# A DLRM tower on one core: transposes of both tiles in a row, then both Grams, with layer matmuls among them

## The chip, the cores and the metric

The kernel runs on one core of a Trainium2 chip. Its engines run side by side and meet through semaphores: PE (matrix products), DVE and ACT (element-wise work and evictions from PSUM), POOL (here it issues gathers) and SP (here it issues the other DMAs). The metric is the time of one execution on the device in microseconds (us), lower is better.

## What is computed

For each of 2048 rows of the batch, 27 ids each pick a row of 128 floats from a table of their own. The 27 vectors give all pairwise dot products (351), a dense context of 16 values is appended, and three layers follow:

```python
e = jnp.stack([tbl_0[ids[:, 0]], ..., tbl_26[ids[:, 26]]], axis=1)
dot = jnp.einsum('bnd,bmd->bnm', e, e)      # 27 x 27 per row of the batch
z = flat[:, idx]                            # its 351 entries below the diagonal
h = jnp.concatenate([z, dense_ctx], axis=1)
h = jnp.maximum(h @ W_top1 + b_top1, 0.0)   # 367 -> 512
h = jnp.maximum(h @ W_top2 + b_top2, 0.0)   # 512 -> 256
y = h @ W_top3                              # 256 -> 1
```

Ten of the tables have 1000 rows; the others have 1250, 12500 or 125000.

## The kernel before

The batch is worked off in eight pairs of tiles, a tile being 128 rows of the batch. `sweep` writes three bodies: pair 0 unrolled, a hardware loop over pairs 1 to 6 (its passes), and pair 7 unrolled. A pair goes through these stages.

*Lookups.* The ten tables of 1000 rows (`NM`) live in SBUF as `parts`, a high and a low half of each float (`split_high` on ACT, `split_low` on DVE), and are read by a matrix product with a onehot of the ids. `make_onehot` builds one table's onehot in eight instructions from `ids_b`, mostly on DVE, for pair 0 partly on ACT (`ACT_ONEHOTS`). There are four onehot slots (`OH`), so tables 4 to 9 wait for lookups that free a slot. `lookup(p, k)` does two tables into one PSUM bank (five per pair), and ACT moves the bank to `embT`.

*Gathers.* The other 17 tables (`NG`) are gathered by POOL, 17 gathers of 128 rows per tile, at most two queued at a time, into `rows`. There is one buffer per tile, so the gathers of a group for pair p+1 wait until PE has transposed that group of pair p.

*Transposes.* The 17 blocks of a tile are transposed by PE in five groups (`TR`, of 4, 4, 4, 3, 2 blocks; `transpose_rows`) into the four `emb_ps` banks, which the lookups use too, and moved to `embT` by ACT (groups 0, 2, 4) and DVE (groups 1, 3).

*Gram.* `gram(p, t, s)` does half a tile's Gram matrices: 64 small products, into one bank per half. DVE copies the first half and ACT the second (`keep_blocks`), and DVE's `turn` makes `z` of a tile. PE transposes it (`transpose_z`), and the layers follow, one pair behind: in the loop they stand among the next pair's stages (`layers`). In the profile a float32 product counts as two records, each with its own weight load.

*SP* loads the tables, the weights, the ids of the onehots (`load_ids`: tables 0 to 3, then 4 to 9; each goes to all 128 partitions, 128 KB per table) and the ids of the gathers (`load_idx`, one per tile). In the loop the ids of tables 4 to 9 of the next pair are loaded when DVE has built this pair's ten onehots, and `load_idx(p + 1, 1)` when all rows of tile 1 have landed.

Each engine works its list in the order in which the code writes it; nothing reorders it. PE's list for a pair in the loop is: lookup 0, `transpose_z` of the pair before (tile 1), lookups 1 and 2, the first layer of the pair before, lookups 3 and 4; then per tile the five groups, a layer (the second beside tile 0, the third beside tile 1), a wait for the moves, and the Gram. `transpose_z` of tile 0 ends it.

## Time and profile before

| | |
|---|---|
| time, median of 3 runs | 417.63 us (416.83 to 418.69) |
| the profiled execution: time | 419.41 us |
| its span | 417.6 us |
| PE, DVE, ACT, POOL busy | 83%, 66%, 38%, 63% of the span |
| mean granted clock of PE | 0.95 |

The span is what the trace covers, from the first to the last instruction; the time has 1.8 us around it. "Idle before" in a row is the time its engine stood still ahead of the row, with what ended it; "issue" means that nothing which the profile shows held it. A pair's stage is best found by PE's first lookup of the pair, at 80.98, 128.91, 172.43 and so on to 352.15 us for pairs 1 to 7.

### The profile page before, as it was taken

How to read it: one execution, taken by the hardware profiler on the slowest of the kernel's cores; microseconds unless marked ns; L12 is line 12 of the kernel's file. 1: busy time of each engine (PE TensorE's matmuls, PEld its weight loads, DVE VectorE, ACT ScalarE, POOL GpSimd, SP SyncE). 2: the span in 40 equal slices, each digit the busy share in tenths (PEclk: the TensorE clock that was granted, in tenths of full speed). 3: DMA queues.
4: the chain of work that ended last, by engine and by line, in shares of the span. 5: the costliest groups of instructions: out<-in, count | busy, mean ns of one | idle time of the engine just before them, and what ended most of it. 6: DMA issues, size and time to landing. Idle time of an engine off the chain costs nothing.

```text
span 417.6 us, 15062 instructions
## 1 busy us (share of the span) xinstructions
PE 348.4 (83%) x6092; PEld 312.5 (75%) x6092; DVE 276.0 (66%) x741; ACT 159.7 (38%) x221; POOL 262.4 (63%) x277
## 2 busy tenths in 40 slices
PE   0277686799979998899989998999899998899766
PEld 0266576689859897789778986898688976897565
DVE  0647954796765965896579677787479748952410
ACT  0827961223432334422442343334422334234422
POOL 5777417777477737677777767767777677770000
PEclk9978675999998999999999999999999999999889
DMA  4799995362425233245524352419333562210000
GB/s 82 176 254 249 222 82 85 65 99 64 99 54 110 52 74 84 58 90 71 113 58 102 58 111 52 109 32 85 98 75 82 66 108 56 54 53 14 3 3 0
DMA packets 29611, 35.51 MB, mean 85 GB/s; under 512 B 12729, under 2 KB 23617, under 8 KB 29586
## 3 DMA queue, kind: packets, MB, share of 16 engines
q1 hardware_dynamic: 20882, 17.32, 26.6%
q0 software_dynamic: 8704, 17.84, 15.7%
q8 instruction: 18, 0.29, 0.3%
q14 instruction: 7, 0.06, 0.0%
HBM read 35.13 MB, written 0.01 MB: 84 GB/s over the span
## 4 chain that ended last, share of the span: by engine, by line
PE 61%; DVE 12%; issue 10%; DMA 7%; ACT 6%; SPq 4%; ACTq 0%; DVEq 0%
PE emb_ps L579 26%; PE gram_ps L602 13%; DVE onehot L474 10%; PE mlp_ps L628 9%; PE mlp_ps L636 6%; DMA blocks<-in_tbl 4%; ACT embT L366 4%; PE emb_ps L591 3%; DMA ids_b<-in_ids_mm 3%; SPq L223 2%; PE mlp_ps L664 2%; PE mlp_ps L669 1%; DVE embT L480 1%; PE mlp_ps L612 1%; ACT h L408 1%
## 5 line engine op out<-in xcount | busy, mean ns | idle before, releaser
L333 POOL DMA_INDIRECT rows<-in_tbl,idx x272 | 262.1, 964 | 113.5 <-DMA rows<-in_tbl,idx 76.8
L474 DVE TENSOR_SCALAR onehot<-ids_b,row_of 128x256 fp32r<-128x256 int32 x616 | 188.5, 381 | 40.4 <-PE emb_ps L579 25.1
L579 PE MATMUL emb_ps<-onehot,parts 125*128 125x256 f32 x1280 | 171.4, 295 | 35.4 <-ACT parts L345 24.0
L579 PEld LDWEIGHTS emb_ps<-onehot,parts 125*128 125x128 f32 x1280 | 163.9, 200 | 40.1 <-ACT parts L345 24.7
L362 ACT ACTIVATE embT<-emb_ps 128x512 f32<-128x512 f32 x40 | 48.0, 1216 | 107.3 <-PE emb_ps L579 107.3
L602 PE MATMUL gram_ps<-embT 128*32 128x26 f32 x4096 | 56.8, 198 | 20.0 <-issue 11.6
L602 PEld LDWEIGHTS gram_ps<-embT 128*32 128x32 f32 x4096 | 47.7, 112 | 33.8 <-issue 28.3
L480 DVE COPY embT<-emb_ps 128x512 f32<-128x512 f32 (+1 forms) x32 | 31.2, 1052 | 32.2 <-PE emb_ps L591 32.2
L591 PE MATMUL emb_ps<-ident,rows 128*128 128x128 f32 x272 | 40.4, 294 | 8.1 <-ACT embT L366 7.7
L366 ACT ACTIVATE embT<-emb_ps 128x512 f32<-128x512 f32 (+1 forms) x48 | 44.6, 1076 | 1.1 <-PE emb_ps L591 1.1
L591 PEld LDWEIGHTS emb_ps<-ident,rows 128*128 128x128 f32 x272 | 32.2, 150 | 13.6 <-ACT embT L366 6.7
L391 ACT ACTIVATE blocks<-gram_ps 128x416 f32<-128x416 f32 x16 | 14.5, 909 | 69.5 <-PE gram_ps L602 69.5
L628 PE MATMUL mlp_ps<-zT,w_sb 128*128 128x256 f32 (+1 forms) x168 | 37.5, 378 | 0.0
L628 PEld LDWEIGHTS mlp_ps<-zT,w_sb 128*128 128x128 f32 (+1 forms) x168 | 31.3, 189 | 4.2
L377 ACT ACTIVATE h<-mlp_ps,b_sb 128x256 f32<-128x256 f32 x42 | 17.6, 470 | 39.8 <-PE mlp_ps L628 22.2
L486 DVE COPY blocks<-gram_ps 128x416 f32<-128x416 f32 x16 | 14.0, 874 | 24.7 <-PE gram_ps L602 24.6
L494 DVE STREAM_TRANSPOSE turned<-blocks 128x832 f32<-128x832 f32 x16 | 16.6, 1040 | 14.3 <-ACT blocks L391 14.2
L636 PE MATMUL mlp_ps<-h,w_sb 128*128 128x256 f32 x112 | 25.3, 380 | 0.0
L636 PEld LDWEIGHTS mlp_ps<-h,w_sb 128*128 128x128 f32 x112 | 20.8, 191 | 2.5
L509 DVE COPY z<-turned 128x351 f32<-128x351 f32 x16 | 9.5, 596 | 1.7
L354 ACT ACTIVATE onehot<-ids_b,row_of 128x256 fp32r<-128x256 int32 x24 | 9.9, 493 | 0.0
L461 DVE TENSOR_TENSOR parts<-turned,parts 125x1024 fp32r<-125x1024 f32 x6 | 7.2, 1235 | 2.5 <-ACT parts L345 2.5
(34 smaller groups left out, 95.9 us busy)
## 6 DMA issues: line engine op xcount, KB each, us to landing
ids_b<-in_ids_mm SPq DMA_DIRECT2D x8, 768.0 KB
rows<-in_tbl,idx POOLq DMA_INDIRECT x272
ids_b<-in_ids_mm SPq DMA_DIRECT2D x8, 512.0 KB
turned<-in_tbl SPq DMA_DIRECT2D x6, 448.0 KB
h<-in_tbl SPq DMA_DIRECT2D x2, 448.0 KB
blocks<-in_tbl SPq DMA_DIRECT2D x2, 448.0 KB
w_sb<-in_W_top SPq DMA_DIRECT2D x1, 512.0 KB, 6.0
w_sb<-in_W_top SPq DMA_DIRECT2D x2, 224.0 KB
```

Source lines behind the costliest of these rows:

```text
L333: pool.indirect_dma_start(rows[:, t, n, :], None, tables[f], bass.IndirectOffsetOnAxis(idx[:, t, f:f + 1], 0), engine_sem=gathers_written) ...
L362: nc.scalar.activation(*lookup_views(k), ACT.Copy).then_inc(emb_act, 1)
L366: nc.scalar.activation(*row_views(t, k), ACT.Copy).then_inc(emb_act, 1)
L377: last = nc.scalar.activation(dst[:, n, :], mlp_ps[job % 2][:, m * W:(m + 1) * W], ACT.Relu, bias=bias[:, n:n + 1])
L474: last = nc.vector.tensor_scalar(onehot[:, k % OH, c, :], ids_b[:, k, :], row_of[:, c:c + 1], None, ALU.is_equal)
L480: nc.vector.tensor_copy(*row_views(t, k)).then_inc(emb_dve, 1)
L494: nc.vector.transpose(turned[:, t, 0:NJ * G], blocks[:, t, :, :].rearrange("p j g -> p (j g)")).then_inc(s_turned, 1)
L579: last = nc.tensor.matmul(emb_ps[BANK[k]][:, m * W:(m + 1) * W], parts[0:MP, f, part, c * D:(c + 1) * D], onehot[0:MP, f % OH, c, :], star ...
L591: done = nc.tensor.transpose(bank[:, m * P:(m + 1) * P], rows[:, t, n, :], ident[:])
L602: last = nc.tensor.matmul(gram_ps[s][q * COLS:(q + 1) * COLS, g * NJ:(g + 1) * NJ], embT[:, t, at:at + COLS], embT[:, t, at:at + NJ], star ...
L628: last = nc.tensor.matmul(mlp_ps[job % 2][:, m * W:(m + 1) * W], w1_sb[0:K1[c], c, n * P:(n + 1) * P], zT[0:K1[c], c, :], start=(c == 0), ...
L636: last = nc.tensor.matmul(mlp_ps[0][:, m * W:(m + 1) * W], w2_sb[:, n, m * P:(m + 1) * P], h1[:, n, :], start=(n == 0), stop=(n == N1 - 1))
```

## The change

Four things change together.

1. In each pair PE transposes all ten groups of both tiles first, and only then does both Grams. The wait for the moves stands ahead of each Gram. ACT's and DVE's lists follow.
2. In the loop, half of the first layer (six calls) stays after lookup 2. The other six calls and the eight of the second layer go to the Grams: `FIRST_CALLS` of them ahead of a tile's Gram, the others after the groups of `CALLS_AT`. The third layer comes after both Grams. In the last pair the layers stay whole.
3. In pair 0 the last two onehot tables (`EARLY`) are not looked up. POOL gathers their rows for both tiles (four gathers, between the tiles' own), and PE transposes them (`transpose_early`). Their onehots are not built for pair 0. The tables are still loaded for the later pairs. PE waits for `ident` alone, which is loaded ahead of table 4, and no longer for all constants.
4. The ids of the onehot tables come in three parts (0-1, 2-3, 4-9). Those of pair 1 are asked for ahead of the weights. In pair 0 DVE moves the rows first and builds the first four onehots of pair 1 between its Gram steps.

```diff
-ACT_ONEHOTS = (3, 6, 9)
+ACT_ONEHOTS = (3, 6)
+EARLY = range(NM - LOOK_TABLES, NM)
+BUILT = NM - len(EARLY) - len(ACT_ONEHOTS)
...
-IDS = [range(0, OH), range(OH, NM)]
+IDS = [range(0, 2), range(2, OH), range(OH, NM)]
+FIRST_CALLS = [3, 4]
+CALLS_AT = [(8, 16, 24), (3, 7, 11, 15)]
+
+def ids_part(k):
...
         ids_b = sb("ids_b", [P, NM, W], I32)
-        y = sb("y", [1, W], F32)
+        y = sb_view(early_rows, 0, [[1, W]], 0, 1)
...
+                done = max(OH, IDS[h].stop)
                 if isinstance(p, int) and p == 0:
-                    done = IDS[h].stop
+                    done = min(done, EARLY.start)
                     sp.wait_ge(onehot_act, sum(f < done for f in ACT_ONEHOTS))
                     sp.wait_ge(s_onehot, done - sum(f < done for f in ACT_ONEHOTS))
                 else:
-                    sp.wait_ge(s_onehot, p * NM - len(ACT_ONEHOTS) + IDS[h].stop)
+                    sp.wait_ge(s_onehot, BUILT + (p - 1) * NM + done)
...
             load_ids(0, 1)
             load_table(2)
             load_table(3)
+            load_ids(0, 2)
+            sp.dma_start(ident[:], ident_in).then_inc(s_ident, 16)
             for k in range(STAGES, NM):
...
                 load_table(k)
-            sp.dma_start(ident[:], ident_in).then_inc(s_const, 16)
+            for h in range(2):
+                ids_read(0, h)
+                load_ids(1, h)
             for c in range(KCH):
...
-                if not last:
-                    ids_read(p, 0)
-                    load_ids(p + 1, 0)
+                if not last and not first:
+                    for h in range(2):
+                        ids_read(p, h)
+                        load_ids(p + 1, h)
...
+                        if first:
+                            sp.wait_ge(s_early, 16 * TILES * len(EARLY))
                         load_idx(p + 1, t)
                         if t == 0:
-                            ids_read(p, 1)
-                            load_ids(p + 1, 1)
+                            ids_read(p, 2)
+                            load_ids(p + 1, 2)
...
+                extra = 0 if first else TILES * len(EARLY)
                 for t in range(TILES):
...
+                            one_queued((p * TILES + t) * NG + n + (TILES * len(EARLY) if first and t else extra))
+                    if first and t == 0:
+                        pool.wait_ge(s_idx[1], 16)
+                        for t2 in range(TILES):
+                            for n, k in enumerate(EARLY):
+                                f = MM_TABLES[k]
+                                one_queued(NG + t2 * len(EARLY) + n)
+                                pool.indirect_dma_start(early_rows[:, t2, n, :], None, tables[f],
+                                                        bass.IndirectOffsetOnAxis(idx[:, t2, f:f + 1], 0),
+                                                        engine_sem=gathers_written
+                                                        ).then_inc(s_early, 16)
...
-            make_onehot(ACT_ONEHOTS[2])
...
                         layers(p - 1, 1)
+                        if last:
+                            layers(p - 1, 2)
                 for t in range(TILES):
                     for k in range(NT):
                         if not BY_DVE[row_job(t, k)]:
                             move_rows(p, t, k)
+                for t in range(TILES):
                     if not first:
-                        layers(p - 1, 2 + t)
+                        layers(p - 1, (3 if last else 2) + t)
                     if last and t:
                         last_layers("z", 0)
                     keep_blocks(p, t, 1)
                 if not last:
+                    if not first:
+                        layers(p - 1, 4)
                     move_z(p, 0)
...
-                if k not in ACT_ONEHOTS:
+                if k not in ACT_ONEHOTS and k not in EARLY:
                     make_onehot(0, k)
                 split_low(k)
...
+                if not last and not first:
                     make_onehot(p + 1, 2)
                     make_onehot(p + 1, 3)
                 for t in range(TILES):
                     for k in range(NT):
                         if BY_DVE[row_job(t, k)]:
                             move_rows(p, t, k)
+                for t in range(TILES):
                     if t:
                         turn(p, 0)
-                    if not last:
+                    if not last and not first:
                         make_onehot(p + 1, t)
                     keep_blocks(p, t, 0)
+                    if first:
+                        make_onehot(p + 1, 2 * (1 - t))
+                        make_onehot(p + 1, 2 * (1 - t) + 1)
                 turn(p, 1)
...
-                    pe.wait_ge(s_onehot, p * NM - len(ACT_ONEHOTS) + max(OH, (k + 1) * LOOK_TABLES))
+                    pe.wait_ge(s_onehot, BUILT + (p - 1) * NM + max(OH, (k + 1) * LOOK_TABLES))
...
+            def transpose_early():
+
+                bank_free(0, LOOK - 1)
+                pe.wait_ge(s_ident, 16)
+                pe.wait_ge(s_early, 16 * TILES * len(EARLY))
+                for n in range(len(EARLY)):
+                    for t in range(TILES):
+                        done = nc.tensor.transpose(emb_ps[BANK[LOOK - 1]][:, n * W + t * P:n * W + (t + 1) * P],
+                                                   early_rows[:, t, n, :], ident[:])
+                done.then_inc(emb_filled, 1)
...
+            def gram(p, t, s, between=None):
                 past(pe, (gram_dve, gram_act)[s], p * TILES + t)
...
                                                 start=True, stop=True)
+                    if between and GS * s + g in CALLS_AT[t]:
+                        between(p - 1, FIRST_CALLS[t] + CALLS_AT[t].index(GS * s + g))
                 last.then_inc(gram_filled, 1)
...
-                    pe.wait_ge(s_const, 16 * 5)
-                    for job in (2, 3):
...
+            def first_layer(p, half, call):
+
+                job, m, c = 2 + half, call // KCH, call % KCH
+                if call == 0:
+                    pe.wait_ge(mlp_moved, BANKS + p * MLP_JOBS + 2)
+                n = 2 * half + m
+                done = nc.tensor.matmul(mlp_ps[job % 2][:, m * W:(m + 1) * W],
+                                        w1_sb[0:K1[c], c, n * P:(n + 1) * P], zT[0:K1[c], c, :],
+                                        start=(c == 0), stop=(c == KCH - 1))
+                if call == 2 * KCH - 1:
+                    done.then_inc(mlp_filled, 1)
...
+            def second_layer(p, call):
+
+                m, n = call // N1, call % N1
+                if call == 0:
+                    pe.wait_ge(mlp_moved, BANKS + p * MLP_JOBS + 4)
+                done = nc.tensor.matmul(mlp_ps[0][:, m * W:(m + 1) * W], w2_sb[:, n, m * P:(m + 1) * P], h1[:, n, :],
+                                        start=(n == 0), stop=(n == N1 - 1))
+                if call == N2 * N1 - 1:
+                    done.then_inc(mlp_filled, 1)
...
+            def lookups(p, first, last):
+                for k in range(LOOK):
+                    if first and k == LOOK - 1:
+                        transpose_early()
+                    else:
+                        lookup(p, k)
+                    if not first and k == 0:
+                        transpose_z(p - 1, 1)
+                    if not first and k == 2:
+                        pe.wait_ge(s_w1, 16 * sum(1 + (n % 16 > 0) for n in K1))
+                        pe.wait_ge(s_const, 16 * 4)
+                        for call in range(2 * KCH):
+                            first_layer(p - 1, 0, call)
+                        if last:
+                            for call in range(2 * KCH):
+                                first_layer(p - 1, 1, call)
...
-                for k in range(LOOK):
-                    lookup(p, k)
-                    if not first and k == 0:
-                        layers(p - 1, 0)
-                    if not first and k == 2:
-                        layers(p - 1, 1)
+                lookups(p, first, last)
                 if first:
-                    pe.wait_ge(s_const, 16 * 5)
+                    pe.wait_ge(s_ident, 16)
                     pe.wait_ge(s_pad, 2)
                 for t in range(TILES):
                     for k in range(NT):
                         transpose_rows(p, t, k)
-
-                    if not first:
-                        layers(p - 1, 2 + t)
-
-                    done = [row_job(t, k) for k in range(NT)]
-                    wait_moved(pe, p, max(j for j in done if BY_DVE[j]))
-                    wait_moved(pe, p, max(j for j in done if not BY_DVE[j]))
-                    gram(p, t, 0)
-                    if last and t:
-                        last_layers("z", 0)
-                    gram(p, t, 1)
+                for t in range(TILES):
+                    layer = (first_layer_rest, second_layer)[t]
+                    if first:
+                        emb_moved(p, t)
+                        gram(p, t, 0)
+                        gram(p, t, 1)
+                    elif not last:
+                        for call in range(FIRST_CALLS[t]):
+                            layer(p - 1, call)
+                        emb_moved(p, t)
+                        gram(p, t, 0, layer)
+                        gram(p, t, 1, layer)
+                    else:
+                        if t == 0:
+                            for call in range(N2 * N1):
+                                second_layer(p - 1, call)
+                        else:
+                            third_layer(p - 1)
+                        emb_moved(p, t)
+                        gram(p, t, 0)
+                        if t:
+                            last_layers("z", 0)
+                        gram(p, t, 1)
+                if first:
+
+                    pe.wait_ge(s_low, NM)
+                elif not last:
+                    third_layer(p - 1)
                 if not last:
                     transpose_z(p, 0)
```

PE's list in the loop, from the last lookup to tile 1's transposes. `emb_ps0` to `emb_ps3` are the banks of lookups and transposes, `gram_ps0` and `gram_ps1` those of the Gram halves, and x64 counts the small products. Before:

```order
L579 MATMUL emb_ps0<-onehot,parts 128x256 x32
L591 MATMUL emb_ps1<-ident,rows 128x128 x4
L591 MATMUL emb_ps2<-ident,rows 128x128 x4
L591 MATMUL emb_ps3<-ident,rows 128x128 x4
L591 MATMUL emb_ps0<-ident,rows 128x128 x3
L591 MATMUL emb_ps1<-ident,rows 128x128 x2
L636 MATMUL mlp_ps0<-h1,w2_sb 128x256 x8
L602 MATMUL gram_ps0<-embT 32x26 x64
L602 MATMUL gram_ps1<-embT 32x26 x64
L591 MATMUL emb_ps2<-ident,rows 128x128 x4
L591 MATMUL emb_ps3<-ident,rows 128x128 x4
```

The change, the same engine and place, from tile 1's third group of transposes on:

```order
L647 MATMUL emb_ps0<-ident,rows 128x128 x4
L647 MATMUL emb_ps1<-ident,rows 128x128 x3
L647 MATMUL emb_ps2<-ident,rows 128x128 x2
L677 MATMUL mlp_ps1<-zT,w1_sb 128x256 x3
L656 MATMUL gram_ps0<-embT 32x26 x36
L677 MATMUL mlp_ps1<-zT,w1_sb 128x256
L656 MATMUL gram_ps0<-embT 32x26 x28
L656 MATMUL gram_ps1<-embT 32x26 x4
L677 MATMUL mlp_ps1<-zT,w1_sb 128x256
L656 MATMUL gram_ps1<-embT 32x26 x32
L677 MATMUL mlp_ps1<-zT,w1_sb 128x256
L656 MATMUL gram_ps1<-embT 32x26 x28
```

Tile 1's transposes have moved from behind tile 0's Gram to ahead of it, and calls of the first layer (L677) have come in between.

DVE's list in pair 0, from its last table split to the first turn into `z`. `onehot` rows here are those for pair 1. Before:

```order
L461 TENSOR_TENSOR parts<-turned,parts 125x1024 x2
L474 TENSOR_SCALAR onehot<-ids_b,row_of 128x256 x16
L480 COPY embT<-emb_ps2 128x4x128
L480 COPY embT<-emb_ps0 128x3x128
L474 TENSOR_SCALAR onehot<-ids_b,row_of 128x256 x8
L486 COPY blocks<-gram_ps0 128x16x26
L480 COPY embT<-emb_ps3 128x4x128
L480 COPY embT<-emb_ps1 128x3x128
L494 STREAM_TRANSPOSE turned<-blocks 128x832
```

The change:

```order
L502 TENSOR_TENSOR parts<-turned,parts 125x1024 x2
L521 COPY embT<-emb_ps2 128x4x128
L521 COPY embT<-emb_ps0 128x3x128
L521 COPY embT<-emb_ps3 128x4x128
L521 COPY embT<-emb_ps1 128x3x128
L527 COPY blocks<-gram_ps0 128x16x26
L515 TENSOR_SCALAR onehot<-ids_b,row_of 128x256 x16
L535 STREAM_TRANSPOSE turned<-blocks 128x832
```

The moves of rows now stand ahead of the onehots, and sixteen onehot instructions stand between the first Gram copy and tile 0's turn.

## Rows read from the trace of the kernel before

**Rows 1.** Page: engine shares; two groups (busy us, mean ns, idle before).

```profile
PE 348.4 (83%) x6092; PEld 312.5 (75%) x6092; DVE 276.0 (66%) x741; ACT 159.7 (38%) x221; POOL 262.4 (63%) x277
...
L377 ACT ACTIVATE h<-mlp_ps,b_sb 128x256 f32<-128x256 f32 x42 | 17.6, 470 | 39.8 <-PE mlp_ps L628 22.2
L486 DVE COPY blocks<-gram_ps 128x416 f32<-128x416 f32 x16 | 14.0, 874 | 24.7 <-PE gram_ps L602 24.6
```

**Rows 2.** Stretches: us, busy PE, PEld, DVE, ACT, POOL; clock; DMA share, GB/s.

```profile
80.98:128.91 47.93, 42.36 (x758) 37.85 (x757) 33.47 (x94) 16.97 (x23) 32.60 (x36) 0.97 0.42 79
128.91:172.43 43.52, 40.22 (x756) 36.21 (x755) 32.99 (x94) 16.21 (x23) 28.05 (x30) 1.00 0.33 74
172.43:352.15 179.72, 166.89 (x3025) 148.30 (x3025) 136.76 (x377) 65.81 (x88) 132.99 (x139) 1.00 0.42 81
352.15:417.60 65.45, 53.93 (x849) 48.97 (x847) 26.77 (x66) 22.34 (x39) 18.65 (x20) 0.95 0.09 23
```

**Rows 3.** Timeline of PE, the loop's sixth pass: start, us, line, count [idle before].

```profile
332.94 2.09 PE L591 MATMUL emb_ps<-ident,rows 128*128 128x128 f32 x15
...
335.78 3.62 PE L636 MATMUL mlp_ps<-h,w_sb 128*128 128x256 f32 x16
339.33 4.27 PE L602 MATMUL gram_ps<-embT 128*32 128x26 f32 x256
343.55 1.83 PE L591 MATMUL emb_ps<-ident,rows 128*128 128x128 f32 x15
...
347.62 4.22 PE L602 MATMUL gram_ps<-embT 128*32 128x26 f32 x256 [0.21 <-ACT embT L366]
```

**Rows 4.** Timeline of the weight loads, Grams of the second and third pass.

```profile
168.98 2.32 PEld L602 LDWEIGHTS gram_ps<-embT 128*32 128x32 f32 x256 [0.70 <-issue]
...
205.67 0.58 PEld L602 LDWEIGHTS gram_ps<-embT 128*32 128x32 f32 x55 [0.19 <-issue]
```

**Rows 5.** Timeline, POOL: first gather of pair 1, last of 4, first of 7.

```profile
61.16 1.11 POOL L333 DMA_INDIRECT rows<-in_tbl,idx  x1 [12.93 <-PE emb_ps L591]
...
241.35 0.94 POOL L333 DMA_INDIRECT rows<-in_tbl,idx  x1 [0.30 <-issue]
...
334.44 0.94 POOL L333 DMA_INDIRECT rows<-in_tbl,idx  x1 [1.60 <-issue]
```

**Rows 6.** Timeline, SP: ids load and next idx load, first and fourth pass.

```profile
100.29 0.37 SPq L238 DMA_DIRECT2D ids_b<-in_ids_mm  x1
112.61 0.35 SPq L250 DMA_DIRECT2D idx<-in_ids  x1
...
236.32 0.37 SPq L238 DMA_DIRECT2D ids_b<-in_ids_mm  x1
...
249.84 0.34 SPq L250 DMA_DIRECT2D idx<-in_ids  x1
```

**Rows 7.** DMA queues (packets, MB, share) at 238 to 245; at 246 to 250.

```profile
q1 hardware_dynamic: 506, 0.52, 48.6%
...
q0 software_dynamic: 259, 0.54, 44.0%
```

**Rows 8.** Timeline of PE and DVE in the first pair.

```profile
52.39 6.34 PE L579 MATMUL emb_ps<-onehot,parts 125*128 125x256 f32 x32 [2.39 <-ACT embT L362]
...
57.16 4.29 DVE L474 TENSOR_SCALAR onehot<-ids_b,row_of 128x256 fp32r<-128x256 int32 x16 [5.24 <-DMA ids_b<-in_ids_mm]
...
63.33 2.89 PE L602 MATMUL gram_ps<-embT 128*32 128x26 f32 x166 [1.84 <-DVE embT L480]
```

**Rows 9.** Stretches: DVE turning a tile into z; PE, clock, after a stop.

```profile
353.40:355.70 2.30, 2.10 (x4) 1.00 0.24 57
...
126.17:129.20 3.03, 3.03 (x126) 0.50 0.45 86
```

**Rows 10.** Timeline of PE, the last pair: two stops in Grams.

```profile
388.23 1.31 PE L602 MATMUL gram_ps<-embT 128*32 128x26 f32 x95 [2.35 <-issue]
...
397.84 1.24 PE L602 MATMUL gram_ps<-embT 128*32 128x26 f32 x123 [1.54 <-issue]
```

61 lines of the change are left out of this document (24 added, 37 removed).

## The prediction

> **What bounds the kernel now.** I read the engines' shares first: PE is busy 83%, no other engine over 66% [rows 1], so PE is the first suspect. The table by stage [rows 2] then cuts the span at each pair's first lookup: 81.0 us for the first pair (the rest of the span), 47.9 for the first pass of the loop, 43.5 for the second, 179.7 for the next four (44.9 each), 65.5 for the last pair. PE is busy 167 of those 179.7 us. PE's timeline of one pass [rows 3] shows the phases that the change moves: tile 0's transposes (from T0 = 332.94), 2.84 us later the second layer, then Gram of tile 0, and transposes and Gram of tile 1. Each Gram holds PE 4.2 us.
>
> Two things run close behind PE. POOL issues one gather each 1.25 us (0.94 busy, 0.30 idle), 34 per pair = 42.5 us, and the next pair's first gather starts 1.5 us after T0 [rows 5]. And the DMA queues: in each pass SP loads six tables' ids (768 KB) as soon as DVE has built the ten onehots, 19.3 us after the first lookup. From that issue to the idx load that waits for tile 1's last rows are 12.3 us in the first pass and 13.5 in the fourth [rows 6], though the fourth's last gather was issued 8.5 us before that point [rows 5]. The DMA rows say why: from 238 to 245 all 506 packets are of SP's queue and none of the gathers', whose 259 packets come from 246 to 250 [rows 7]. So rows gathered while the ids load runs arrive 12 to 13.5 us after its issue. Before, that cost nothing: tile 1's last group was wanted 13 us after T0 (end of its transposes, [rows 3]).
>
> **The change, part by part.** L is a pass's first lookup.
>
> *Grams with matmuls among them.* The fastest Gram's 256 weight loads took 2.32 us with no gap; in another they stop 0.19 us, run 0.58 for 55, stop again [rows 4], 4.2 us in all [rows 3]. The fast one and the first stretch of the others come right after slow matmuls, so I read the gaps as a supply of instructions that falls behind a burst. A layer call lasts 0.45 us (3.62 for 8, [rows 3]); one after each 64 or 32 small records lets the supply catch up. Bounds: nothing saved, or both Grams at 2.4 (3.6 saved). I take 3.15 each, as even ungapped stretches run slower than the fastest and tile 1's second half has no call in it: 2.1 saved. The calls themselves are moved, not added.
>
> *Waits on PE.* The wait for tile 1's eviction goes (0.21, [rows 3]): all moves are done before any Gram. A new one comes: the rest of the first layer ends at group 24 of tile 0's Gram, ACT then needs two ReLUs (0.47 each, [rows 1]) before the second layer, and 7 groups of Gram cover about 0.6 of 1.1 us: +0.5. Behind it stand the second layer and tile 1's Gram. The 34 transposes stay paced by ACT's moves, twice 2.84 and a little, say 5.9. ACT's and DVE's other moved steps have slack: DVE's onehot 1 of the next pair ends some 2 us before the lookup that wants it; without that slack it would be up to 1 us. A pass without other waits is 44.9 - 2.1 - 0.2 + 0.5 = 43.1; I take **43.2**, just above POOL's 42.5.
>
> *Rows wanted early.* Half of the first layer (six calls, 2.7 us) leaves the stretch ahead of T0, so T0 = L + 23.0, with the ids load at L + 19.2. Tile 1's last group is now wanted at T0 + 5.7. Where its gathers fall behind the ids load they arrive at L + 31.5 to 32.7 = T0 + 8.5 to 9.7: a **wait of 2.8 to 4.0 us** on PE, with the rest of the first layer, both Grams and all that follows behind it. It depends on the pass before: the last gather is issued 1.6 + 41.2 us after that pass's T0, which is 46.7 - P after the ids load, P being that pass's length. After P = 43.2 it is 3.5 late and the group waits; after P over 47 it slips in ahead. A wait costs more than itself: behind a stop of 2.15 us the granted clock was 0.50 (1.2 GHz) for 3.0 us, in which 126 records ran [rows 9], half the fastest Gram's number [rows 4]; I take 1.5. So passes alternate between 43.2 + 3.2 + 1.5 = 47.9 and 43.2, or settle near 45.5: mean **45.55**. Pass 2 has no wait (below). Passes 2 to 6 take 43.2 + 4 x 45.55 = 225.4 against 43.5 + 179.7 = 223.2: **+2.2**. SP's other loads (ids of four tables in two parts, idx) keep their places.
>
> On this wait a rule of the Trainium skill speaks the other way. "DMA: Bandwidth & Descriptors", section "Issuing engines are not separate DMA queues", says that DMAs of different engines run on the same 16 engines and interleave. The trace disagrees: none of 506 packets [rows 7]. By the page the gathers would keep landing and this term would be nothing, which is rival B.
>
> *First pair.* Before, the last two tables' lookups began after a bank wait of 2.39 and took 6.3 us, DVE waited 5.24 for ids and built 16 onehots in 4.29 before it moved rows, and the Gram began at 63.33 [rows 8]. Now four gathers and four transposes replace those lookups, ACT builds one onehot less before its moves, DVE moves rows at once. The lookups before them end near 50.0 (52.39 - 2.39) as before; the ids in three parts delay ACT's first onehot, which I price at nothing since that stage waits for tables (up to 2 us if not). The 38 transposes, paced by ACT, end near 57.5. POOL's last gather ended at 48.2 (61.16 - 12.93); four more make 53.2, and they should land by 57.5, as weights and not ids lie ahead of them in SP's queue. So the Gram begins at **58.2**. PE's wait for all constants, now for `ident` alone, ended nothing before and saves nothing. Code stops in the Gram stay, so that PE ends near 71.4, but DVE is later: half a Gram 2.5, its copy 0.9 [rows 1], 16 onehot instructions 4.3 [rows 8] to 4.9, turning tile 0 into z 2.3 [rows 9], the second copy 0.9, 16 onehots. 58.2 + 15.2 to 16.4 with small gaps gives the first lookup at 74 to 75.2, **74.6** against 80.98: **-6.4**. Bounds: 72 (PE's end) and 82.4 (rival D).
>
> *First pass of the loop.* 43.2; code stops 2.2 (two fall into the Grams; bounds 0 and 3); its gathers start near 59.5, not 74.6, so the last is issued near 100, 6 us behind the ids load at 93.8, and the wait is 3.8; clock 1.5. 50.7 against 47.9: **+2.8**. That length is also why pass 2 has no wait.
>
> *Last pair.* No ids load, so no wait for rows; transposes in a row cost what they did apart. Stops for code (2.35, 1.54, [rows 10]) fall at other places: from the stop that ends at 388.23 to the one that ends at 397.84 are 504 instructions, and from half of those on to the next arrival 3.7 us. With that spacing carried over to the new order I get 1.1 less; bounds 1.5 less and 2 more. **-1.1**.
>
> Sum: -6.4 + 2.8 + 2.2 - 1.1 = -2.5. The profiled execution has a span of 417.6 and a time of 419.41, 1.8 more; its changed span would be 415.1 and its time 416.9. The median of the runs shown is 417.63, so in their terms it is **415.1**.
>
> **Rivals.**
> B, rows come in time: passes of 43.2, the first 45.4. From 74.6 to 120.0, to 336.0, and 64.4 for the last pair: 400.4. For it: only part of a group may be late. Against: [rows 7].
> C, slower: the wait with its clock loss in every pass. It needs an ids load that holds back gathers issued shortly before it too, so that a long pass does not help the next. Passes 2 to 6 then take 43.2 + 2.8 + 1.5 = 47.5, 12.1 above my 225.4: 427. The kernel is slower than before from a mean pass of 46.2 on. For it: the delay grew from 12.3 to 13.5 [rows 6]. Against: gathers issued well ahead landed.
> D: in the first pair the last gathers land only after the second ids load, near 65; the Gram begins at 65.5, the first lookup is at 82.4: 423.
> E: the calls save nothing in the Grams: passes near 46.9, the second and first 2 longer: 424.
> F: the wait exists but stays under 1.5 us and costs no clock: passes of 44, 407.5.
>
> **How the numbers follow.** Forecast 0.48 (own range 411 to 420), B 0.08, F 0.14, C 0.10, D 0.09, E 0.11. 0.5% is 2.1 us, about what a measurement of this kernel can tell from no change. Of the forecast's case 0.27 lies below 415.5, 0.17 within, 0.04 above 419.7. With B and F faster is 0.49; with a part of E (0.03) same is 0.20; the rest, slower, 0.31. The range reaches from F's lower side to E: 405 to 424, which leaves B and C out.
>
> **What the profile of after would show.** Right: PE waiting for DMA rows before tile 1's fourth or fifth group, some 3 us in every other pass or so, a lower clock behind it; Grams with few gaps; the loop's first lookup near 74.6; passes of 43 to 48. Wrong: no such wait (B), Grams as long as before beside the calls (E), the first Gram after 62 (D), a mean pass over 46.2 (C).

## The result and the profile after

The changed kernel is slower: 428.79 us (median of four runs, 425.99 to 432.82) against 417.37 (four runs, 416.83 to 418.69). The ratio is 1.025, with a 95% interval of 1.018 to 1.031. Ratios here and below compare fast runs alone, and the run of 432.82 us is a slow one. The forecast was 415.1 us with a range of 405 to 424, so the time lies outside it, on the other side of the kernel before. The profiled execution has a span of 427.7 us and a time of 429.53.

The stages of the changed kernel, cut at each pair's first lookup as in [rows 2] (us of the stretch, then busy time and number of instructions of each engine, granted clock of PE, DMA share, GB/s). The first line is the first pass of the loop, the last line the last pair:

```profile
core 0: us, PE busy (x) PEld busy (x) DVE busy (x) ACT busy (x) POOL busy (x), PEclk, DMA share, GB/s
82.39:128.54 46.15, 43.78 (x756) 37.60 (x757) 33.43 (x94) 15.57 (x20) 28.60 (x31) 0.96 0.36 75
128.54:177.36 48.82, 43.34 (x760) 36.61 (x758) 34.32 (x94) 16.43 (x23) 35.31 (x38) 0.97 0.38 77
177.36:221.28 43.92, 41.84 (x760) 35.85 (x758) 33.87 (x94) 16.38 (x23) 28.46 (x31) 1.00 0.34 76
221.28:270.72 49.44, 43.50 (x760) 36.87 (x758) 34.48 (x94) 16.53 (x23) 36.58 (x39) 0.97 0.42 79
270.72:314.86 44.14, 41.98 (x760) 35.97 (x758) 33.54 (x94) 16.37 (x23) 27.00 (x29) 1.00 0.39 72
314.86:365.66 50.80, 44.10 (x759) 37.44 (x757) 35.03 (x94) 16.53 (x23) 38.53 (x41) 0.93 0.46 80
365.66:427.70 62.04, 50.78 (x850) 45.95 (x848) 26.45 (x66) 21.72 (x40) 12.27 (x13) 1.00 0.07 17
```

| | before | forecast | after |
|---|---|---|---|
| first pair, to the loop's first lookup | 80.7 | 74.6 | 82.4 |
| first pass | 47.8 | 50.7 | 46.1 |
| passes 2 to 6 | 223.6 | 225.4 | 237.1 |
| last pair | 65.5 | 64.4 | 62.0 |

The column of the kernel before differs a little from [rows 2]: PE's first lookups of pairs 1 and 2 begin at 80.74 and 128.56, not at 80.98 and 128.91.

```profile
80.74 4.37 PE L579 MATMUL emb_ps<-onehot,parts 125*128 125x256 f32 x32
...
128.56 4.33 PE L579 MATMUL emb_ps<-onehot,parts 125*128 125x256 f32 x32
```

Against the forecast the first pair lost 7.8 us and passes 2 to 6 lost 11.7; the first pass and the last pair gave 4.6 and 2.3 back. Passes 2, 4 and 6 are long, 3 and 5 are short.

PE's waits show what the long stretches hold (line waited for: us in total, times, longest):

```profile
PE emb_ps L647 <- DMA rows<-in_tbl,idx: 22.9, 6, 8.9
PE gram_ps L656 <- issue: 10.5, 7, 2.0
```

Before, PE never waited for rows. PE's timeline gives the start, the length, the operation, and in brackets the idle time before it with what ended it. The longest wait stands in pair 0, ahead of tile 1's last two transposes; the second one shown is that of pass 4, with what follows it:

```profile
65.91 0.66 PE L647 MATMUL emb_ps<-ident,rows 128*128 128x128 f32 x2 [8.85 <-DMA rows<-in_tbl,idx]
66.50 2.78 PE L656 MATMUL gram_ps<-embT 128*32 128x26 f32 x175
...
252.93 0.94 PE L647 MATMUL emb_ps<-ident,rows 128*128 128x128 f32 x5 [3.93 <-DMA rows<-in_tbl,idx]
253.66 2.77 PE L677 MATMUL mlp_ps<-zT,w_sb 128*128 128x256 f32 x6
```

The six layer records behind the second wait take 2.77 us at a granted clock of 0.50 (1.2 GHz); in a pass without a wait they take 1.46 or 1.47. SP's rows of the same two places (ids load, then the idx load that follows when all rows of tile 1 are there):

```profile
53.79 0.38 SPq L252 DMA_DIRECT2D ids_b<-in_ids_mm  x1
65.86 0.35 SPq L265 DMA_DIRECT2D idx<-in_ids  x1
...
240.43 0.37 SPq L252 DMA_DIRECT2D ids_b<-in_ids_mm  x1
253.38 0.35 SPq L265 DMA_DIRECT2D idx<-in_ids  x1
```

POOL issued pair 0's last gather at 53.64, ahead of that ids load. Still it landed only behind it: from 56 to 63 us the DMA view has packets of SP's queue alone, none of the gathers' (q0):

```profile
## 3 DMA queue, kind: packets, MB, share of 16 engines
q1 hardware_dynamic: 547, 0.56, 39.7%
```

### The profile page after: what moved, and what is told of

It is laid out like the page before. It is cut to its first block, busy times and chain, and to the rows that moved or that the text cites. A ratio compares the mean times of both kernels' runs of the same rounds, so it can differ in the third digit from the quotient of the medians.

```text
span 427.7 us, 15034 instructions
## 1 busy us (share of the span) xinstructions
PE 343.9 (80%) x6064; PEld 296.2 (69%) x6064; DVE 275.6 (64%) x733; ACT 153.8 (36%) x212; POOL 265.4 (62%) x281
## 4 chain that ended last, share of the span: by engine, by line
PE 43%; DMA 34%; issue 11%; DVE 8%; ACT 3%; POOLq 0%; POOL 0%; DVEq 0%; ACTq 0%; SPq 0%
DMA rows<-in_tbl,idx 33%; PE emb_ps L624 18%; PE mlp_ps L677 7%; DVE onehot L515 7%; PE gram_ps L656 7%; PE mlp_ps L691 5%; PE emb_ps L647 2%; ACT embT L402 2%; PE mlp_ps L720 1%; DMA early_rows<-in_tbl,idx 1%; PE mlp_ps L699 1%; PE mlp_ps L725 1%; ACT h L444 1%; ACT h L413 0%; PE mlp_ps L668 0%
## 5 line engine op out<-in xcount | busy, mean ns | idle before, releaser
L515 DVE TENSOR_SCALAR onehot<-ids_b,row_of 128x256 fp32r<-128x256 int32 x608 | 185.3, 381 | 22.4 <-PE emb_ps L624 15.3
L624 PE MATMUL emb_ps<-onehot,parts 125*128 125x256 f32 x1248 | 161.9, 289 | 37.9 <-ACT parts L381 26.0
L624 PEld LDWEIGHTS emb_ps<-onehot,parts 125*128 125x128 f32 x1248 | 154.9, 194 | 41.5 <-ACT parts L381 27.9
L398 ACT ACTIVATE embT<-emb_ps 128x512 f32<-128x512 f32 x40 | 47.9, 1218 | 110.0 <-PE emb_ps L624 107.4
L656 PE MATMUL gram_ps<-embT 128*32 128x26 f32 x4096 | 55.4, 198 | 11.5 <-issue 10.5
L647 PEld LDWEIGHTS emb_ps<-ident,rows 128*128 128x128 f32 x272 | 29.7, 142 | 37.0 <-issue 28.4
L677 PE MATMUL mlp_ps<-zT,w_sb 128*128 128x256 f32 (+1 forms) x168 | 46.9, 415 | 0.0
L677 PEld LDWEIGHTS mlp_ps<-zT,w_sb 128*128 128x128 f32 (+1 forms) x168 | 31.6, 203 | 4.2
L691 PE MATMUL mlp_ps<-h,w_sb 128*128 128x256 f32 x112 | 32.4, 407 | 1.9 <-ACT h L413 1.9
L691 PEld LDWEIGHTS mlp_ps<-h,w_sb 128*128 128x128 f32 x112 | 18.7, 189 | 4.6 <-ACT h L413 2.5
L381 ACT ACTIVATE parts<-turned 125x1024 fp32r<-125x1024 f32 x6 | 6.2, 1050 | 10.0 <-DMA turned<-in_tbl 10.0
```

The lines of the kernel that those rows point to most:

```text
L398: nc.scalar.activation(*lookup_views(k), ACT.Copy).then_inc(emb_act, 1)
L515: last = nc.vector.tensor_scalar(onehot[:, k % OH, c, :], ids_b[:, k, :], row_of[:, c:c + 1], None, ALU.is_equal)
L624: last = nc.tensor.matmul(emb_ps[BANK[k]][:, m * W:(m + 1) * W], parts[0:MP, f, part, c * D:(c + 1) * D], onehot[0:MP, f % OH, c, :], star ...
L647: done = nc.tensor.transpose(bank[:, m * P:(m + 1) * P], rows[:, t, n, :], ident[:])
L656: last = nc.tensor.matmul(gram_ps[s][q * COLS:(q + 1) * COLS, g * NJ:(g + 1) * NJ], embT[:, t, at:at + COLS], embT[:, t, at:at + NJ], star ...
L677: done = nc.tensor.matmul(mlp_ps[job % 2][:, m * W:(m + 1) * W], w1_sb[0:K1[c], c, n * P:(n + 1) * P], zT[0:K1[c], c, :], start=(c == 0), ...
```

## The theories and the experiments

Theory S: the one load of 768 KB, ids of tables 4 to 9, keeps everything else from moving while it runs, and PE's new waits are all of its making. Its rival is G: the gathers themselves can't come earlier. Later come theory C, that the load holds back blocks of code too, and P against Q, on what slows a Gram. The letters B and C in the expectations are not those of the prediction's rivals.

### The load behind the rows, and a chip on which nothing can be told of it

```diff
                         load_idx(p + 1, t)
-                        if t == 0:
+                        if t == 1:
                             ids_read(p, 2)
                             load_ids(p + 1, 2)
```

Four kernels ran on a first chip: this edit to the changed kernel; the same edit to the kernel before; the edit in the loop alone; and the changed kernel with `FIRST_CALLS = [6, 8]` and `CALLS_AT = [(), ()]`, that is with the calls whole.

> The changed kernel with one edit: SP asks for the ids of tables 4 to 9 of the next pair (768 KB) only after all rows of tile 1 have landed, in every pair but the last. Theory S (that load keeps the gathers' queue from moving, and the rows that PE waits for are those caught behind it): the waits of 8.9 us in pair 0 and of 3.5, 3.9 and 4.6 us in passes 2, 4 and 6 go, with the lower clock behind them. Loop passes are 44 us each, the first lookup of the loop comes near 75 instead of 82.4, and the time is 428.8 - 7.5 - 17 = 404 us (400 to 410). Rival G (the rows are late because the gathers themselves, issued one each 1.25 us by POOL and written through one queue, can't be faster): the waits stay as they are, 425 to 430 us. Rival O (the load is only moved onto another path: its ids now reach DVE too late for tables 4 and 5 of the next pair): row waits go, but PE waits for onehots at lookups 2 and 3, 412 to 425 us.

> The kernel before with the same edit: the ids of tables 4 to 9 of the next pair are asked for behind the wait for tile 1's rows. Theory S says that the rows landed in time there anyway, since they are wanted 13 us and not 5.7 us after the first transpose: the time stays within 0.5% of 417.4, and only the landing of the last rows moves, from 12 to 13.5 us behind the ids load to within 7 us of the last gather's issue. If the held-back rows cost something hidden in the kernel before as well, it is 3 to 8 us faster. If the later load reaches DVE too late, it is slower.

> The changed kernel with the same edit in the loop's six passes alone; in pair 0 the ids load stays ahead of tile 1's rows. Theory S: the wait of 8.9 us in pair 0 stays, the loop's first lookup stays near 82.4, the waits in the loop go: 428.8 - 17 = 412 us (408 to 415), so that the distance to the kernel with the edit everywhere is the price of pair 0's wait, 7 to 9 us. Rival: if the waits in the loop are a consequence of pair 0's late start, this one has them still, and the time is above 420.

> The changed kernel with the layer calls put back in one piece ahead of the Grams: all six of the rest of the first layer before tile 0's Gram, all eight of the second before tile 1's, none inside a Gram. If the calls let the supply of instructions catch up, as the prediction held, the two Grams of a pass go from 3.0 back to 4.2 us each, the calls from 0.63 back to 0.45 us each (1.3 us per pass given back for 7 calls), and a pass gets 0.8 to 1.2 us longer: 433 to 436 us, if the waits for rows stay as they are. If the calls in the Gram earn nothing net, it is 425 to 429 us.

On this chip the kernel before took 702 us, not 417, in each of 19 runs. The four measured 723.9, 701.7, 723.5 and 703.8 us: ratios 1.031, 1.001, 1.030 and 1.003. None of the expectations applies, since PE never waits for rows here: it is late everywhere. PE's timeline of the kernel before with the edit shows where, in pair 3, tile 0:

```profile
329.39 0.44 PE L602 MATMUL gram_ps<-embT 128*32 128x26 f32 x29
...
348.04 0.20 PE L602 MATMUL gram_ps<-embT 128*32 128x26 f32 x1 [1.88 <-issue]
348.75 3.07 PE L602 MATMUL gram_ps<-embT 128*32 128x26 f32 x210 [0.51 <-issue]
```

and POOL's, the last gather before a pause:

```profile
344.63 0.94 POOL L333 DMA_INDIRECT rows<-in_tbl,idx  x1 [0.30 <-issue]
```

A Gram takes 22 us instead of 4: behind the first 29 of its 256 records, 17 come in ones and threes, up to 1.9 us apart, and the other 210 in 3.07 us. The turn comes 4.1 us after POOL's last gather began. In the last pair, where POOL issues none, the Grams run as usual. The large matmuls of the lookups and layers keep their length (4.03 us for 32). So these runs say nothing on S, but they pose a question on the forecast's first term: is a Gram slowed by a burst of small matmuls, or by POOL's gathers? With layer calls among the Grams it was 20 us slower than with the calls whole (723.5 against 703.8); those two kernels also differ in the place of the load, which by itself did nothing to the kernel before on this chip (1.001). The edit in the loop alone was not measured on another chip.

The first kernel was run again:

> The same kernel as in the first of the experiments: the changed kernel, with the ids of tables 4 to 9 of the next pair asked for behind the wait for tile 1's rows. There the kernel before itself took 702 us instead of 417, because each Gram took some 22 us instead of 4.2 while POOL was writing gathers, so that no wait for rows could arise and nothing was told about it. Where the kernel before takes about 417 us, theory S expects 404 us (400 to 410), with no wait of PE for rows, passes of 44 us and the loop's first lookup near 75; rival G (the gathers themselves are the limit) expects 425 to 430 with the waits as they were; rival O (the ids come too late for DVE) expects 412 to 425 with waits for onehots. Where the kernel before takes about 702 us again, it is 3% slower than that one, as measured.

413.75 us (four runs, 412.91 to 414.46) against 418.05; ratio 0.989, 0.986 to 0.991. Passes 2 to 6 took 43.90, 43.91, 43.88, 44.04 and 43.96, 219.7 us in all instead of 237.1, with no wait for rows. This is the 17 us of theory S, and G falls. The time lies in the range of rival O, but the waits for onehots in these passes are 0.94 to 1.02 us, as in the changed kernel (0.91 to 0.98), so O falls too. Theory S had 400 to 410: the first pair and the first pass gave less than expected. The Gram of pair 0 began at 57.35 instead of 66.50, yet the loop's first lookup came at 78.83, and the first pass took 51.4. PE's timeline of it:

```profile
57.35 2.55 PE L656 MATMUL gram_ps<-embT 128*32 128x26 f32 x175
64.00 2.15 PE L656 MATMUL gram_ps<-embT 128*32 128x26 f32 x127 [4.09 <-issue]
71.42 2.24 PE L656 MATMUL gram_ps<-embT 128*32 128x26 f32 x128 [5.28 <-issue]
75.16 1.57 PE L656 MATMUL gram_ps<-embT 128*32 128x26 f32 x82 [1.49 <-issue]
...
117.28 0.42 PE L656 MATMUL gram_ps<-embT 128*32 128x26 f32 x12 [3.76 <-issue]
```

The same three stops of pair 0 are 1.24, 1.46 and 1.89 us in the changed kernel, at the same instructions (behind 175, 127 and 128 records). They are stops for code: by the DMA view, one microsecond at a time, a block of 16 KB on the instruction queue (q8) moves in the microsecond from 67, 71 and 75 in the changed kernel and from 61, 68 and 72 here, and PE goes on 2 to 3.5 us later each time. The load, issued at 57.42, now runs beside them.

### The load behind tile 0's Gram

```diff
                         load_idx(p + 1, t)
-                        if t == 0:
+                        if t == 1:
+                            sp.wait_ge(gram_filled, p * TILES * STEPS + STEPS)
+                            sp.sem_inc(sp_waited, 1)
                             ids_read(p, 2)
                             load_ids(p + 1, 2)
```

> The changed kernel with the load of the ids of tables 4 to 9 of the next pair moved further: behind tile 1's rows and behind tile 0's Gram, in every pair but the last. With the load only behind the rows the time was 413.75 us; passes 2 to 6 took 43.9 us each with no wait for rows, but in pair 0 PE stood 4.09, 5.28 and 1.49 us in the Grams for nothing that the profile shows (10.9; 4.6 in the changed kernel), and 3.76 us in the first pass's Gram, each time while or just after that load ran. Theory C (the load holds back the blocks of code that PE's first Grams wait for, as it held back the gathers): behind tile 0's Gram most of it goes, the loop's first lookup comes at 73 to 76 instead of 78.8, the first pass takes 47 to 48 instead of 51.4, and the time is 405 to 409 us. Rival: these stops are the price of code that is asked for late, whatever the queues hold: they stay, 412 to 415 us. Rival L: the ids now come too late for DVE (tables 4 and 5 are wanted some 8 us after the next pair's first lookup): passes get longer than 44.5, 414 or more.

417.85 us (ten runs, 415.87 to 421.07) against 419.38; ratio 0.998, 0.994 to 1.002. That is worse than the run before it, and outside what theory C (405 to 409) and its first rival (412 to 415) expected; the other rival, late ids, wanted passes over 44.5, and there are none. The first lookup came at 77.40 (73 to 76 expected) and the first pass took 55.45 (47 to 48 expected). Yet C's mechanism is there all the more plainly. The stops before the load are back at their old size, and one of 8 us stands wherever the load now runs:

```profile
61.14 2.20 PE L658 MATMUL gram_ps<-embT 128*32 128x26 f32 x127 [1.28 <-issue]
65.03 2.16 PE L658 MATMUL gram_ps<-embT 128*32 128x26 f32 x128 [1.69 <-issue]
75.34 1.58 PE L658 MATMUL gram_ps<-embT 128*32 128x26 f32 x82 [8.15 <-issue]
...
129.27 1.46 PE L658 MATMUL gram_ps<-embT 128*32 128x26 f32 x88 [8.41 <-issue]
```

SP issued the loads at 62.69 and 114.64. Blocks of code moved at 58, 62, 73, and at 110, 113, 126: none in the ten microseconds of either load, the next in its last. (With the load right behind the rows, one block still moved 3.6 us after the load's issue, the next seven us after that.) The expectation took it that PE had its code by then; it hadn't. Passes 2 to 6 have no such stop and take 43.9 to 44.5 again.

Beside it, the calls whole:

> The kernel of the run beside it (ids behind tile 0's Gram), with the layer calls in one piece: all six of the rest of the first layer ahead of tile 0's Gram, all eight of the second ahead of tile 1's, none in a Gram. Without waits for rows the value of putting calls into the Grams can be read. The prediction held that they save 2.1 us of Gram per pass, less 0.5 for a ReLU; measured were 0.63 instead of 0.45 us per call (1.3 for seven). If both hold, a pass of the loop is 0.3 to 1.1 us longer with the calls whole, and the time 2 to 7 us longer. If a Gram is slowed not by a lack of calls but by POOL writing gathers at the same time (the one fast Gram of the kernel before, 2.32 us, lay where POOL stood still), the Grams are 4.2 us each here too, since POOL writes gathers in them: the same 2 to 7 us. If the calls in the Grams earn nothing: within 1 us of the run beside it.

420.59 us, 1.007 (1.002 to 1.011), 2.7 us more than with the calls in the Grams. But it isn't the passes that are longer: 2 to 6 take 220.6 against 220.3 us, although DVE's onehots hold PE 1.1 to 2.1 us in each (0.95 with the load behind the rows). It is in the first pair (1.0 us), whose code is the same in both and whose stop beside the load is 9.58 instead of 8.15 us, and in the first pass (1.35 us), whose stop is 8.41 us in both; so it says nothing of the calls. The two Grams took 3.65 and 3.86 us in pass 5.

### The load in six pieces

```diff
-                sp.dma_start(ids_b[:, a:b, :], src.partition_broadcast(P)).then_inc(s_ids[h], 16)
+                for j, f in enumerate(range(a, b)):
+                    sp.dma_start(ids_b[:, f:f + 1, :], ids_mm[f:f + 1, bass.ts(p, W)].partition_broadcast(P)
+                                 ).then_inc(s_ids[h], 16)
+                    if f + 1 < b and not (isinstance(p, int) and p == 0):
+                        sp.wait_ge(s_ids[h], p * 16 * (b - a) + 16 * (j + 1))
+                        sp.sem_inc(sp_waited, 1)
```

This is for part 2; parts 0 and 1 stay single loads, and DVE and ACT wait for six landings of part 2. It stands in the changed kernel's own place, ahead of tile 1's rows.

> The changed kernel with one edit: the ids of tables 4 to 9 of the next pair are asked for at the same place as in it, but as six loads of 128 KB, each of which SP asks for only when the one before has landed. Same bytes, same queue, same engine. Theory S+C (one long load keeps everything behind it from moving: the gathers' rows and the blocks of code): between pieces both move. The waits for rows in passes 2, 4 and 6 go, pair 0 keeps at most 2 us of its 8.9, its stops for code stay at 4 to 6 us, so the loop's first lookup is at 75 to 78; the first pass takes 46 to 48, passes 2 to 6 take 43.9 each, the last pair 62.5: 404 to 410 us. Rival B (bytes count, not the length of the load): the waits shrink to a third or so but stay in every other pass, 415 to 425. Rival L: six loads one after the other take so long that DVE waits for ids: passes over 44.5.

407.35 us (407.06 to 407.48), 0.975 (0.968 to 0.982): as expected by S and C together, 21 us below the changed kernel. This expectation's rival B, that bytes count and not the length of the load, falls: the same bytes are loaded. So does its rival L, as the waits for onehots in passes 2 to 6 stay at 0.93 to 1.05 us. The six loads are spread over more time, though: from the first issue to the last it is 17.7 us in the first pass. No run has six loads without the waits between them, so how much the cutting does, and how much the waiting, is not shown. Passes 2 to 6 take 43.99, 43.93, 43.87, 44.03 and 43.93, and no stop of pair 0, for rows or for code, is over 1.7 us:

```profile
54.97 0.88 PE L659 MATMUL emb_ps<-ident,rows 128*128 128x128 f32 x3 [1.60 <-DMA rows<-in_tbl,idx]
56.30 0.66 PE L659 MATMUL emb_ps<-ident,rows 128*128 128x128 f32 x2 [0.45 <-DMA rows<-in_tbl,idx]
56.88 3.04 PE L668 MATMUL gram_ps<-embT 128*32 128x26 f32 x175
61.48 2.10 PE L668 MATMUL gram_ps<-embT 128*32 128x26 f32 x127 [1.55 <-issue]
64.78 2.08 PE L668 MATMUL gram_ps<-embT 128*32 128x26 f32 x128 [1.20 <-issue]
68.52 1.53 PE L668 MATMUL gram_ps<-embT 128*32 128x26 f32 x82 [1.66 <-issue]
```

The loop's first lookup is at 72.78, below the 75 expected, with stops for code of 4.4 us in all. The transposes also begin earlier, at 43.94 instead of 48.75, but that gained nothing: they then wait for rows, and the Gram begins at 56.88, as in the kernels whose transposes begin late (56.5 to 57.6). The first pass takes 49.6, longer than expected: its first lookup takes 6.06 us instead of 4.03, at a mean granted clock of 0.63, behind a wait of 1.90 for a onehot; a stop for code takes 1.54, and half of the second layer behind it 3.52 instead of 1.99, at 0.55.

Half the load at once asks the same by its size. From pair 1 on, the ids of tables 4 to 9 reach 64 of the 128 partitions only; the onehots of the other 64 rows are built from old ids, in the same time:

```diff
-                sp.dma_start(ids_b[:, a:b, :], src.partition_broadcast(P)).then_inc(s_ids[h], 16)
+                n = P // 2 if h == 2 and not (isinstance(p, int) and p == 0) else P
+                sp.dma_start(ids_b[0:n, a:b, :], src.partition_broadcast(n)).then_inc(s_ids[h], 16)
```

> The changed kernel with half of the suspected load: from pair 1 on the ids of tables 4 to 9 go to 64 of the 128 partitions, in the same place and as one load; so the onehots of the other 64 rows of those tables are built from old ids (that part of the computation is wrong, its work is the same). Theory S: the load takes about 5.2 us instead of 10.4, and rows arrive that much earlier. Pair 0's wait of 8.9 shrinks to 3 to 5 us, the waits of 3.5 to 4.6 us in the loop vanish or fall below 1 us, passes 2 to 6 are 44 to 44.5 each: 407 to 416 us. If rows were late for another reason (POOL, the gathers' own queue), nothing moves: 425 to 430.

406.94 us (403.77 to 410.23), 0.977 (0.968 to 0.986). In the loop no wait is left, and passes 2 to 6 take 43.85 to 44.05. Pair 0's wait falls from 8.85 to 0.95 us, with 0.42 before the last group, and the first lookup is at 73.84. That is more than half, and not by size alone: POOL's last gather began 1.07 us ahead of the load here (52.98 and 54.05) and only 0.15 us ahead of it in the changed kernel.

### What a Gram costs

The last experiments set the calls against POOL's gathers. With the load in pieces and the calls whole:

> The kernel beside it (ids in six loads) with the layer calls in one piece ahead of the Grams. In the last comparison of this kind passes were the same length with calls whole, 44.0 against 43.9, but DVE's onehots held PE 1.9 us there and 0.95 with the calls in the Grams, and from the first transpose to the next pair's first lookup it was 20.2 against 20.9. So if the layer calls in the Grams cost more than they save, passes 2 to 6 take 43.0 to 43.4 here, 0.5 to 0.9 less each, and the time is 2 to 5 us below the run beside it. If they save what the prediction held: 2 to 7 us above it.

404.03 us (401.76 to 406.67), 0.969 (0.961 to 0.978), the fastest kernel of the study, though its interval overlaps that of the run beside it. Passes 2 to 6 take 219.2 against 219.75 us, 0.1 less each and not 0.5 to 0.9: the calls in the Grams cost as much as they save. Most of the rest of the difference is in the first pass (47.2 against 49.6) and in the last pair (61.3 against 63.6), whose code is the same in both; so it is no proof that calls should be whole. Two Grams of this kernel, in pass 4:

```profile
238.26 4.00 PE L668 MATMUL gram_ps<-embT 128*32 128x26 f32 x256
242.19 3.72 PE L703 MATMUL mlp_ps<-h,w_sb 128*128 128x256 f32 x16
245.84 3.95 PE L668 MATMUL gram_ps<-embT 128*32 128x26 f32 x256
```

Then POOL was held until both Grams were done:

```diff
+                if not first:
+                    pool.wait_ge(gram_filled, p * TILES * STEPS)
+                    pool.sem_inc(pool_waited, 1)
                 for t in range(TILES):
                     pool.wait_ge(s_idx[t], (p + 1) * 16)
```

> The changed kernel with the ids load behind tile 0's Gram, calls whole, and POOL held: it starts the next pair's gathers only when both Grams of this pair are done, so that in the loop no gather is written while PE works on a Gram (it will be much slower, since the rows come late: passes of some 60 us). Wanted is the length of a Gram. Theory P (POOL writing gathers is what slows PE's supply of small matmuls: 3.65 and 3.86 us per Gram with POOL at work, calls whole; 22 us on the first chip): from pass 2 on each Gram takes 2.3 to 2.5 us. Theory Q (the supply falls behind a burst of 256 small records by itself): 3.6 to 4.2 us as before. The clock may be lower behind the long waits; then the number of stops within a Gram tells it, none by P and three to six by Q.

The time was 524.1 us, as it had to be. POOL stood still from 247.9 to 265.2 there (pass 3):

```profile
247.00 0.94 POOL L364 DMA_INDIRECT rows<-in_tbl,idx  x1 [0.31 <-issue]
265.21 0.94 POOL L364 DMA_INDIRECT rows<-in_tbl,idx  x1 [17.27 <-issue]
```

and PE's Grams in that time, with the second layer between them:

```profile
255.44 2.54 PE L661 MATMUL gram_ps<-embT 128*32 128x26 f32 x256
257.91 3.72 PE L696 MATMUL mlp_ps<-h,w_sb 128*128 128x256 f32 x16
261.56 2.38 PE L661 MATMUL gram_ps<-embT 128*32 128x26 f32 x256
```

256 records in 2.38 us without a stop: theory P holds, and Q falls. Of the ten Grams of passes 2 to 6, nine take 2.38 us; the tenth, shown first, takes 2.54 at a granted clock of 0.91. With POOL held no rows move either. The kernel with the load behind tile 0's Gram and the calls whole tells the two apart: its load holds back the gathers' rows, so that in tile 1's Gram POOL writes a gather each 1.25 us but no packet of q0 moves, and the Gram is as slow as the others (pass 2, and the DMA view from 174.2 to 177.8):

```profile
174.21 3.66 PE L658 MATMUL gram_ps<-embT 128*32 128x26 f32 x256
...
q1 hardware_dynamic: 266, 0.27, 74.7%
```

It is so in all five passes (3.66 to 3.86 us). SP's load is not the cause either: the second Gram shown with POOL held ran in 2.38 us beside 212 packets of SP's queue. So POOL's writing of gathers is enough, without their rows moving. The one fast Gram of [rows 4] (168.98, 2.32 us) fits, as POOL writes in its first 0.7 us alone: the kernel before's POOL rows there are

```profile
168.76 0.94 POOL L333 DMA_INDIRECT rows<-in_tbl,idx  x1 [0.30 <-DMA rows<-in_tbl,idx]
171.31 0.95 POOL L333 DMA_INDIRECT rows<-in_tbl,idx  x1 [1.61 <-issue]
```

### The pieces in the kernel before

The edit of the six pieces, made in the kernel before at its own place:

> The kernel before with the one edit that took the changed kernel from 428.8 to 407.4 us: the ids of tables 4 to 9 of the next pair come as six loads of 128 KB, each asked for when the one before has landed, in the old place. It tells whether those 21 us are a gain that any kernel with this load would have had, or the price of a wait that the change had made. Theory S: the rows held back cost nothing before, since tile 1's last group was wanted 13 us after the first transpose; passes 2 to 6 stay at 44.7 us, only stops for code behind the ids load (2.15 and 0.85 us in the first pass, 2.72 in pair 0) may shrink, so the time is 0 to 4 us less than the kernel before. If the load cost something hidden there too, the time is 5 to 15 us less, and the change itself is worth little; if six loads one after the other are in the way, it is longer.

418.23 us, 0.996 (0.991 to 1.000), within the 0 to 4 us expected. Passes 2 to 6 take 223.0 us, as before. The load cost nothing there that shows. So nearly all of the 21 us were the price of waits that the change made. With the same six pieces in both, the changed kernel stands at 0.975 and the kernel before at 0.996: without its waits the change gains some 2%.

## Why the prediction was wrong

The changed span came out 12.6 us above the forecast of 415.1: 7.8 in the first pair, 11.7 in passes 2 to 6, less 4.6 in the first pass and 2.3 in the last pair.

*The first pair* (-6.4 forecast, +1.6 measured). The step that failed is the landing: the last gathers "should land by 57.5, as weights and not ids lie ahead of them in SP's queue". SP's own list of the changed kernel has the ids load for pair 1 right behind tile 0's rows, at 53.79, 0.15 us after the last gather's issue. To be issued ahead of the load did not help: the rows took until 65.9, which is rival D (65.5; first lookup 82.4, 423 us), given 0.09. The kernel before had the sign, in rows that the prediction didn't look at: the first is POOL's last gather of pair 0, the others SP's ids load and the idx load that waits for these rows.

```profile
47.28 0.95 POOL L333 DMA_INDIRECT rows<-in_tbl,idx  x1 [0.30 <-issue]
51.31 0.37 SPq L238 DMA_DIRECT2D ids_b<-in_ids_mm  x1
57.46 0.35 SPq L250 DMA_DIRECT2D idx<-in_ids  x1
```

The last rows landed some 10 us after their gather began, though it was 4 us ahead of the load. With the load moved away it is 4 us (53.00 to 57.01). The rest of this term held: where the load was moved, the Gram began at 57.35 (58.2 forecast), and with six pieces at 56.88; from there to the first lookup it was 15.9 us in the changed kernel and with six pieces, where the forecast had 16.4.

*The first pass* (50.7 forecast, 46.1 measured) followed from that. With the first lookup 7.8 us late, the ids load (102.80) came when all gathers were through; idx followed at 103.75. No wait, and so a short pass.

*Passes 2 to 6* (+2.2 forecast, +13.5 measured). The mechanism was right: waits in every other pass with a lower clock behind them. They began one pass early, because the first pass was short: three long passes and not two, 4.7 us. The long passes took 48.8, 49.4 and 50.8, not 47.9: the waits were 3.5, 3.9 and 4.6 us where I took 3.2, and the base was longer. The short ones took 43.9 and 44.1, not 43.2. That is 7.0 us more, and 4.7 and 7.0 make the 11.7 that were missed. No run supports the prediction's rival C as a whole: a long pass did help the next. But half of its mechanism is there, as the load holds back gathers issued shortly before it too: the one 0.15 us ahead in pair 0 landed 12.3 us after it began, and the one 0.49 us ahead in pass 3 (195.84) 7.0 us after, in time. That C's 427 us are near the measured time is chance. The prediction's rival B (0.08) fell by the row of 547 packets and none of the gathers'. A rule of the Trainium skill spoke for it: "DMA: Bandwidth & Descriptors", section "Issuing engines are not separate DMA queues", says that DMAs of different engines interleave. The trace disagrees there, though not in every stretch: from 196 to 203, in pass 3, 64 packets of the gathers moved beside 412 of SP's.

*The Gram with matmuls among them* (2.1 us saved, less 0.5). The second step that failed is "the calls themselves are moved, not added", which put their price at nothing. With the load in six pieces, and counted from the start of a row to the start of the next, the two Grams of a pass took 6.1 to 6.3 us with the calls in them, as forecast (twice 3.15), and 7.7 to 7.9 with the calls whole: 1.6 saved. But each call costs 0.63 instead of 0.45 us there (1.3 for seven) and a ReLU 0.3. Net: 0.1 us lost, in the two kernels that differ in nothing else. The cause was wrong too. I read the gaps of [rows 4] as a supply that falls behind a burst by itself, because the fast Gram came after slow matmuls; POOL's rows beside it would have shown POOL idle in most of it. This is rival E (0.11) in its outcome, though not in its size, as the row-wise order gained elsewhere: passes went from 44.7 to 43.95 us without waits. That is still 0.75 above the 43.2 of the forecast.

*The last pair* (-1.1 forecast, -3.4 measured): the direction held, the size was under its bound. The stops for code in its Grams were 1.78, 1.75 and 1.99 us, where [rows 10] had 2.35 and 1.54 among others. How much of this the change did is not shown: the same last pair of the kernel before took 62.5 us instead of 65.5 in the run with six pieces, at a mean granted clock of 1.00 instead of 0.95.

The range missed mainly because D and a slower loop were taken as separate cases, each small. They have one cause, the load, and so came together.

## What to carry to other kernels

When a change makes data wanted earlier, look for the longest transfer that can be under way just then, on any queue, and cut it into pieces that wait for each other, as here, or ask for it behind the data; but a long load ahead of unrolled code that PE is still to fetch moves the wait there. Look up in the trace of before when such data lands, and not only when it is asked for. A gap in a run of tiny matmuls is to be read against every engine's rows at that time, POOL's first, before it is put down to PE. Matmuls that move to another place are to be priced there anew. Cases that share a cause belong into one rival, with the chance that they come together.

## What the runs showed of the hardware

A load to 128 partitions on SP's queue (768 KB in some 10 us) held back gathers of POOL's queue for 7 us (0 of 547 packets from 56 to 63) and blocks of code for PE (a stop of 8.15 and one of 8.41 us, where the changed kernel has at most 2.0). It doesn't hold back all of them each time: 64 gather packets moved in 7 us of it in pass 3. In the changed kernel six loads of 128 KB, each waiting for the one before, left no wait for rows over 1.85 us and, in pair 0 and the loop, no stop for code over 1.94, with the calls in the Grams or whole.

POOL writing gathers slows PE's small matmuls: 256 records took 2.38 us with POOL still (2.54 once, at a clock of 0.91), 3.65 to 4.3 with a gather each 1.25 us, also where no rows moved (3.66 to 3.86), and 22 us on one chip, where large matmuls were as fast as elsewhere. Why that chip differs is open. The kernel before took 417.4 to 419.4 us on the others.
